# A fused attention and routed feed-forward kernel: expert weights loaded by SyncE and transposed two jobs a step from the start, routing of the first group and scaling of the first tile cut into pieces

## What is computed

```python
q = x + braak_embed[itok][..., None]                 # (32, 256, 256)
attn = softmax(einsum('bsd,btd->bst', q, side))
o = einsum('bst,btd->bsd', attn, side)
t = o * rsqrt(mean(o * o) + EPS) * norm_w            # 8192 tokens
weights = top2_of_8(softmax(t @ gate_w.T))           # renormalised
h1 = t @ w1.T + 2 * lora(t, a1, b1)                  # F = 1024, rank 16, by expert
h3 = t @ w3.T + 2 * lora(t, a3, b3)
act = silu(h1) * h3
out = x + sum_e weights_e * (act @ w2.T + 2 * lora(act, a2, b2))
```

## Time and profile before

| | |
|---|---|
| times of three runs | 1379.82, 1374.30, 1379.27 us, median 1379.27 |
| span of the profiled execution | 1375.7 us |
| PE busy | 1339.7 us (97%) |
| DVE busy | 890.6 us (65%) |
| ACT busy | 545.8 us (40%) |
| POOL busy | 224.0 us (16%) |
| mean granted TensorE clock | 0.993 of full |

### The profile page before, as it was taken

One profiled execution on the slowest core, in us unless ns is written; L12 is line 12 of the kernel. 1 busy time (PEld: TensorE's weight loads), 2 busy tenths in 40 slices (PEclk: granted clock), 3 DMA queues, 4 the chain that ended last, 5 costly groups with the idle time before them and its releaser, 6 DMA issues.

```text
span 1375.7 us, 18571 instructions
## 1 busy us (share of the span) xinstructions
PE 1339.7 (97%) x6660; PEld 1126.7 (82%) x6660; DVE 890.6 (65%) x1552; ACT 545.8 (40%) x1039; POOL 224.0 (16%) x171
## 2 busy tenths in 40 slices
PE   5999999999999999999999999999999999999997
PEld 4999998888788878887888888887888788888885
DVE  2888874665677566756675667656765676565654
ACT  2877773333333333333342334333433333233332
POOL 1334342020202020202020100101111102020200
PEclk8999999999999999999999999999999999999999
DMA  7434461010101101020202010101010101011000
GB/s 235 130 115 138 145 183 49 0 40 32 39 31 33 39 17 52 1 69 0 69 1 69 0 53 16 38 30 38 30 39 30 38 30 39 30 38 32 0 16 16
DMA packets 59278, 68.88 MB, mean 50 GB/s; under 512 B 7003, under 2 KB 46313, under 8 KB 58985
## 3 DMA queue, kind: packets, MB, share of 16 engines
q1 hardware_dynamic: 54088, 63.27, 14.7%
q10 hardware_dynamic: 5152, 5.11, 1.1%
HBM read 51.27 MB, written 17.10 MB: 50 GB/s over the span
## 4 chain that ended last, share of the span: by engine, by line
PE 80%; DVE 9%; issue 6%; ACT 1%; DMA 1%; ACTq 1%; POOL 0%; SPq 0%; POOLq 0%; DVEq 0%
PE bank L1051 25%; PE bank L1053 24%; PE bank L1052 24%; DVE v_full L937 2%; PE bank L1090 2%; DVE act_s L957 2%; PE bank L1129 2%; DVE act_br L953 1%; PE bank L1234 1%; ACTq L562 1%; PE bank L1135 1%; PE bank L1107 1%; DVE act_b L950 1%; DVE br_lo L965 1%; ACT s_hi L668 1%
## 5 line engine op out<-in xcount | busy, mean ns | idle before, releaser
L942 DVE TENSOR_TENSOR act_a<-silu_a,bank 128x512 f32<-128x512 f32 x128 | 87.9, 687 | 181.8 <-PE bank L1053 164.8
L668 ACT ACTIVATE s_hi<-act_s 128x512 fp32r<-128x512 f32 x128 | 80.9, 632 | 257.2 <-DVE act_s L957 256.3
L963 DVE TENSOR_TENSOR s_lo<-act_s,s_hi 128x512 fp32r<-128x512 f32 x128 | 103.7, 810 | 74.4 <-ACT s_hi L668 74.2
L661 ACT ACTIVATE silu_b<-bank 128x512 f32<-128x512 f32 x128 | 76.3, 596 | 185.9 <-PE bank L1053 184.5
L950 DVE TENSOR_TENSOR act_b<-silu_b,bank 128x512 f32<-128x512 f32 x128 | 88.0, 688 | 72.9 <-PE bank L1053 72.0
L515 POOL TENSOR_TENSOR v_lo<-v_full,v_hi 128x512 fp32r<-128x512 f32 x64 | 94.7, 1512 | 130.5 <-ACT v_hi L653 130.5
L657 ACT ACTIVATE silu_a<-bank 128x512 f32<-128x512 f32 x128 | 76.1, 594 | 92.3 <-PE bank L1053 91.1
L957 DVE TENSOR_TENSOR act_s<-act_a,act_br 128x512 f32<-128x512 f32 x128 | 103.2, 807 | 4.4
L504 POOL TENSOR_TENSOR t_lo<-t_scaled,t_hi 128x1024 fp32r<-128x1024 f32 x16 | 38.5, 2406 | 414.4 <-ACT t_hi L649 414.4
L1051 PE MATMUL bank<-t_hi,w1T_hi 128*128 128x512 f32 x256 | 100.6, 393 | 0.8 <-DVE act_b L950 0.8
L1051 PE MATMUL bank<-s_hi,w2T_hi 128*128 128x512 f32 x256 | 100.4, 392 | 0.2 <-DVE br_lo L965 0.2
(11 more groups left out here) (175 smaller groups left out, 3190.5 us busy)
## 6 DMA issues: line engine op xcount, KB each, us to landing
x_in<-in_x SPq DMA_DIRECT2D x32, 256.0 KB, 2.8
kv<-in_fside_BxSxS SPq DMA_DIRECT2D x32, 256.0 KB, 3.1
t_scratch<-oT SPq DMA_DIRECT2D x32, 256.0 KB, 2.1
t_in<-t_scratch SPq DMA_DIRECT2D x16, 512.0 KB
x_out<-in_x SPq DMA_DIRECT2D x16, 512.0 KB, 3.5
out<-x_out SPq DMA_DIRECT2D x32, 256.0 KB, 2.2
rho<-scale_scratch SPq DMA_DIRECT2D x16, 256.0 KB
rstd<-scale_scratch SPq DMA_DIRECT2D x16, 256.0 KB
```

The lines of the kernel that those rows point to most:

```text
L661: nc.scalar.activation(silu_b[:, :], h1_bank[j % 2][:, :], ACT.Silu).then_inc(silu_b_ready, 1)
L668: nc.scalar.activation(s_hi[j % 2][:, :], act_s[j % 2][:, :], ACT.Copy).then_inc(s_hi_ready, 1)
L942: nc.vector.tensor_tensor(act_a[j % 2][:, :], silu_a[j % 2][:, :], h3_bank[j % 2][:, :], ALU.mult).then_inc(act_a_ready, 1)
L963: nc.vector.tensor_tensor(s_lo[j % 2][:, :], act_s[j % 2][:, :], f32(s_hi[j % 2][:, :]), ALU.subtract)
```

## The change

SP issues the weight loads, in between the loads of the first four sequences, in the order in which the jobs use them, each group with its own semaphore. ACT issues only the two small loads for the bias. The twenty jobs stand two a step in steps 0 to 9. HEAD is now steps 0 to 19, the loop 20 to 27. Routing is cut in ten pieces (eight in steps 10 to 17, the weight's in step 19), behind `probT_low`. The row transposes, the copy and **both tile loads** now stand between step 19 and step 20. Tile 0's scaling stands in halves in steps 28 and 29. For sequence 0, kv is transposed ahead of q.

```diff
-            sp.dma_start(itok_in[:, :], itok.partition_broadcast(STAGES)).then_inc(stage_loaded, 16)
-            sp.dma_start(embed_in[:, :], embed).then_inc(stage_loaded, 16)
             load(0, 0, ring_full=False)
...
-            for c in range(1, RING):
-                load(0, c, ring_full=False)
+            load(0, 1, ring_full=False)
+            sp.dma_start(a1_in[:, :], a1.rearrange("e r d -> (e r) d")).then_inc(a13_loaded, 16)
+            sp.dma_start(a3_in[:, :], a3.rearrange("e r d -> (e r) d")).then_inc(a13_loaded, 16)
+            sp.dma_start(w1_in[:, :, :], w1.rearrange("(p j) d -> p j d", j=FC)).then_inc(w1_loaded, 16)
+            load(0, 2, ring_full=False)
+            sp.dma_start(w3_in[:, :, :], w3.rearrange("(p j) d -> p j d", j=FC)).then_inc(w3_loaded, 16)
+            load(0, 3, ring_full=False)
...
             for c in HEAD[1:]:
                 step(0, c)
-            with sp.Fori(0, LOOPS) as g:
-                for c in LOOP:
-                    step(g, c)
...
             sp.wait_ge(wT_ready, JOBS)
             for k in range(2):
-                sp.wait_ge(t_stored[k], 16)
-            load(0, BATCH - 1)
+                sp.wait_ge(t_stored[k], 32)
             store_rows(0)
             load_tile(0, 0, buffers_used=False)
+            load_tile(0, 1, buffers_used=False)
+            with sp.Fori(0, LOOPS) as g:
+                for c in LOOP:
+                    step(g, c)
+            load(0, BATCH - 1)
             store(0, TAIL[0] - 1)
-            load_tile(0, 1, buffers_used=False)
...
             qk_high(0, 0)
-            load_weights()
...
+            def first_transpose_qk():
+                pe.wait_ge(seq_loaded[0], 32)
+                transpose_seq(kv[0], kT_bank)
+                pe.wait_ge(q_ready, 1)
+                transpose_seq(q[0], qT_bank).then_inc(qkT_ready, 1)
...
             def step(g, c, jobs_here=False, peeled=False):
                 row_max(g, c)
-                if jobs_here:
-                    weight_low(c, 0)
-                if peeled:
-                    beside(c)
                 if not isinstance(g, int) or c + 1 < BATCH:
                     qk_low(g, c + 1)
...
                 probT_low(g, c)
-                if jobs_here:
-                    weight_low(c, 3)
+                if jobs_here and c > 0:
+                    weight_low(jobs_of(c)[1])
+                if peeled:
+                    beside(c)
```

More of the change, by code:

```diff
@@ L282, in adaln_moe_ffn @@
                                    dst[1][:, c, j0 * P:(j0 + 4) * P], nw_at(c))]))
-        FIRST_B_JOB = len(jobs)
+        B_JOB = len(jobs)
         for src, dst in ((b1_by_j, b1T), (b3_by_j, b3T)):
@@ L288, in adaln_moe_ffn @@
                                dst[1][:, j0 * P:(j0 + 4) * P], SCALING)]))
+        W2_JOB = len(jobs)
         for j0 in range(0, FC, 2):
@@ L293, in adaln_moe_ffn @@
                            w2T[1][:, j0:j0 + 2].rearrange("p j d -> p (j d)"), 1.0)]))
+        A2_JOB = len(jobs)
         for j0 in range(0, FC, 4):
@@ L297, in adaln_moe_ffn @@
                            a2T[1][:, j0:j0 + 4].rearrange("p j e -> p (j e)"), 1.0)]))
+        B2_JOB = len(jobs)
         jobs.append(([(128 * c, 128, b2_in[:, c].rearrange("p e r -> p (e r)"), P) for c in range(DC)],
@@ L319, in seq @@
             return 4 * g + c
-        T0_STEP = BATCH - 2
-        HEAD, TAIL = range(0, 12), range(28, 32)
-        LOOP = range(12, 16)
+        HEAD, TAIL = range(0, 20), range(28, 32)
+        LOOP = range(20, 24)
+        T0_STEPS = TAIL[0:2]
         LOOPS = (TAIL[0] - LOOP[0]) // 4
@@ L549, in _, with weight_high @@
         def _(act):
[L550 to L566, removed]
+            def weight_high(n):
                 act.wait_ge(wT_ready, n + 1)
@@ L640, in _ @@
                 step(0, c, c in JOB_STEPS)
-                if c == ROUTE_STEP + 2:
+                if c == ROUTE_STEP + 7:
                     exp_gap(0)
-            with act.Fori(0, LOOPS) as g:
-                for c in LOOP:
-                    step(g, c)
             def t_high(g, c):
@@ L720, in _ @@
             copy_rows(0, row_bank, first=True)
+            with act.Fori(0, LOOPS) as g:
+                for c in LOOP:
+                    step(g, c)
             for c in TAIL:
                 step(0, c)
-                if c == T0_STEP:
+                if c == T0_STEPS[-1]:
                     t_high(0, 0)
@@ L839, in route_second, with route_first, newton, rsqrt_seed @@
                 link(r, 15, nc.vector.tensor_tensor(hots[:, 1].rearrange("p e c -> p c e"), g_hot2[:, :, :], g_hot1[:, :, :], ALU.subtract))
-            def route_rstd(r):
+            def route_first(r):
+                route_copy(r)
+                route_hot1(r)
+            def route_second(r):
+                route_rest(r)
+                route_hot2(r)
+                route_hots(r)
+            def newton(r, n):
+                target = scales[:, 1] if n == 2 else g_y[:, :]
+                link(r, 18 + 3 * n, nc.vector.tensor_tensor(g_t[:, :], g_y[:, :], g_y[:, :], ALU.mult))
+                link(r, 19 + 3 * n, nc.vector.scalar_tensor_tensor(g_t[:, :], g_t[:, :], -0.5, g_z[:, :],
+                                                                   ALU.mult, ALU.mult))
+                link(r, 20 + 3 * n, nc.vector.scalar_tensor_tensor(target, g_t[:, :], 1.5, g_y[:, :],
+                                                                   ALU.add, ALU.mult))
+            def rsqrt_seed(r):
                 y_bits, z_bits = g_y[:, :].bitcast(I32), g_z[:, :].bitcast(I32)
@@ L845, in route_rstd @@
                 link(r, 17, nc.vector.tensor_scalar(y_bits, y_bits, -1.0, RSQRT_SEED, ALU.mult, ALU.add))
+            def route_rstd(r):
+                rsqrt_seed(r)
                 for n in range(3):
[L847 to L852, removed]
+                    newton(r, n)
             def route_gap(r):
@@ L869, in scale_t @@
                     dve.wait_ge(t_lo_ready, tile_no(g, c))
[L870 to L874, removed]
             def load_weight(g, c, buffer_used=True):
@@ L1082, in weight_job, with transpose_seq @@
                 last.then_inc(wT_ready, 1)
+            def transpose_seq(src, dst):
+                for dc in range(DC):
+                    for h in range(SC):
+                        last = nc.tensor.transpose(dst[:, dc * S + h * P:dc * S + (h + 1) * P],
+                                                   src[:, h, dc * P:(dc + 1) * P], ident[:, :])
+                return last
             def transpose_qk(g, c):
                 pe.wait_ge(q_ready, seq(g, c) + 1)
[L1087 to L1090, removed]
-                                                       src[:, h, dc * P:(dc + 1) * P], ident[:, :])
-                last.then_inc(qkT_ready, 1)
+                transpose_seq(q[c % 2], qT_bank)
+                transpose_seq(kv[c % RING], kT_bank).then_inc(qkT_ready, 1)
+            def first_transpose_qk():
[3 more added lines that the diff above has]
+                transpose_seq(q[0], qT_bank).then_inc(qkT_ready, 1)
             def scores(g, c):
@@ L1151, in step @@
                 if jobs_here:
-                    weight_job(c, 1)
+                    weight_job(jobs_of(c)[0])
+                if jobs_here and c == 0:
+                    weight_job(jobs_of(c)[1])
                 if c >= 2:
@@ L1171, in _ @@
                 step(0, c, c in JOB_STEPS)
+            pe.wait_ge(w_lo_ready, JOBS)
+            transpose_rows(0, row_bank)
             with pe.Fori(0, LOOPS) as g:
```

151 lines of the change are left out of this document (98 added, 53 removed).

## The result

| | before | after |
|---|---|---|
| median of 13 runs | 1379.82 us | 1386.44 us |
| lowest and highest | 1374.30, 1384.25 | 1385.08, 1392.02 |
| span of the profiled execution | 1375.7 us | 1383.4 us |

The ratio is 1.0056, with a 95% interval of 1.0041 to 1.0072. The kernel is 0.6% slower. The forecast was 1372.2 us and its range ended at 1377.5: the forecast is wrong in sign.

The account below looks back on a forecast made before the run. PE, busy in 97% of the span, was taken as the bound. Gains of 10.9, 2.1 and 5.2 us less 11.1 lost gave 7.1 us less: span 1368.6, median 1372.2 us, range 1364 to 1377.5.

Parts of the forecast that it names:

- four places: PE's idle or low-clock stretches before stage 2: step 0, the clock after it, routing in steps 9 to 11, stage 1's end.
- The start: Steps 0 and 1: ACT freed of weight transfers, jobs filling PE's wait, scores(2) at 22.4; 10.9 us gained.
- rival 2: The start gains little: SP held by its ring, sequence 4 or the weights late; 1377 us, 13 in 100.
- Routing: Steps 9 to 11 before: cut in pieces behind `probT_low`, its delay of 2.3 us mostly goes; 2.1 us gained.
- The stop in the middle: PE waits 8.2 us for sequence 23, queued behind the tile loads, then 2.9 for the low clock; 11.1 us lost.
- Rival 1: Sequence 23 overtakes the tile loads: stop of 3.8 us, gain 11.5, 1367.8 us; 17 in 100.
- rival 3: Slower than before: stop before step 22 over 22 us, broadcast loads at half their rate; 3 in 100.
- R: The start of the row transposes, 186.11 us before, now the end of step 19; sequence 23's landing forecast at R + 20.2.
- The end of stage 1: Tile 0 scaled earlier: the 2.03 us wait and low clock go, low_rank at 207.5 if undisturbed; 5.2 us gained.

Follow-up runs that it names:

- e1: After with 12 more do-nothing instructions (waits already met) at the start of DVE's list; median 1376.31 us, ratio to before 0.9986.
- e2: Before with 84 more instructions on DVE in step 0, its stage 2 loop then placed as in after; median 1390.08 us, ratio to before 1.0080.
- e5: Before with 60 more instructions on DVE in step 0; median 1379.97 us, ratio to before 1.0007.
- e6: Before with 74 more instructions on DVE in step 0; median 1384.68 us, ratio to before 1.0042.
- e3: After with sequence 23 loaded ahead of rows and tile 0, and tile 1's loads moved behind the loop; median 1373.06 us, ratio to before 0.9960.
- e4: After with the edits of e1 and e3 together; median 1362.63 us, ratio to before 0.9886.
- e7: e4 with row transposes, their copy and both tile loads back behind the loop, tile 0 scaled in step 30; median 1366.17 us, ratio to before 0.9900.

## Why the prediction was wrong

**The step that failed** is a term that the sum hasn't got: stage 2 was put at nothing. The prediction counts four places that can give or lose time, "all before stage 2", and the part on the kernel says of stage 2: "The change leaves this stage as it is." No reason is given beyond that. The text of stage 2 is the same, and so is each instruction of it. Its place in DVE's program is not. The forecast counted the instructions that were moved and those queued behind them, and didn't ask where the loop behind them would stand. This cost 10.4 us in after's profile, and e1, e2, e5 and e6 show it to be the place of DVE's loop alone. Without it after would be at 1376.3, inside the range and 4 us above the forecast.

**The start** was right: 9.57, 16.70 and 22.78 where 9.3, 16.8 and 22.4 were forecast. With four jobs done by then the gain is 31.53 + 1.76 - 22.78 = 10.5 (forecast 10.9). Sequence 4's data did come 1 us later than DVE wanted it (landed at 29.2, wanted at 28.3; forecast 25.5 and 27.5): SP was held in issuing by its queue, as ACT had been (two weights' issues took 4.77 and 3.36 us). That is a piece of rival 2, but next to nothing reached PE.

**Routing**: steps of 5.5 us up to 128.76, as forecast.

**The stop in the middle** had the right place, releaser and cause in SP's order; both sizes were low. It was 9.6 us, not 8.2. `t_in` went out 3.2 us behind the row transposes, as forecast, but sequence 23's kv landed 18.3 us behind it, not 17. The clock came back after 7.4 us of work, not 5.8, so it took 3.7 and not 2.9. Together 13.3 us instead of 11.1. Taking it away gives the same: 12.4 us at the mark from after to e3, and 13.9 from e1 (227.53) to e4. Rival 1, by which sequence 23 would overtake the tiles (a stop of 3.8 us), did not come true. But the sentence under it, "A transfer waits for what was issued on its queue ahead of it", doesn't hold as it stands. Sequence 24's `x_in`, issued at 144.38, landed 5.96 us later at 150.34, and sequence 23's kv, issued ahead of it at 143.09, 7.64 us later at 150.73. So what the Trainium skill says (DMA: Bandwidth & Descriptors, "Queues, rings and completion order"), that a later transfer may complete before an earlier one of its issuer, is seen in this trace; it didn't help sequence 23. When the tiles' own loads landed, the trace doesn't record. In rival 3, the landings for a stop of 15.3 and of 22 us are R + 27.3 and R + 34, with the 0.7 us of DVE that the forecast's own stop has; the chance doesn't hang on it.

**The end of stage 1**: no stop, and full clock, as forecast. Low_rank began 212.70 - 208.53 = 4.2 us earlier, where the sum has 7.1. The missing 2.9 us are 2.2 of the stop, 0.4 of the start, and 0.3 that is spread over the rest. One sign of it: from the probabilities of step 29 to those of step 30 it is 6.12 us (197.36 to 203.48), where a plain step takes 5.52.

**The end of the kernel**: 1.6 us, since PE's clock was low in four of the last six matmuls and in the last transposes. e1 has this too (1.94 us); before, e2, e3, e4, e5 and e6 have not. It doesn't go with the stop in the middle: e7 has no such stop, and its last six matmuls ran at the low clock as well (0.63 us each behind the first). Why the clock falls there in some executions isn't settled; no run tests it.

**The range and the chances.** Slower had 3 in 100, all for a stop of 22 us. An unnamed effect on the stage whose text is untouched had none. The change moved 84 instructions ahead of a loop, and so a share for "something else is shifted" was due.

## What to carry to other kernels

When a change writes out more steps ahead of a hot loop, count the instructions ahead of it, in the built program (here DVE's; no other engine's list was tested), and see whether the body still lies in as few fetch blocks as before. The sign in the profile is idle time marked "issue" at the first instruction of each turn but the first, with more packets on the engine's instruction queue; the remedy cost twelve instructions that do nothing. And before a block of broadcast loads goes into a queue, look for the next plain load that has a due time. Here that load ahead of the block, with half of the block moved to a later place, was worth 13.4 us; the two weren't tried apart. Together with the twelve instructions it makes a kernel 1.1% faster than before.

## What the runs showed of the hardware

- In turns whose jump back went with more packets on the instruction queue, DVE stood 2.4 us behind the jump, and 1.7 us more at a border three or four instructions behind its target (after). With the border ten instructions further on, only the first showed (e6). DVE stands 1.4 us there in any case, so on PE's path this was 2.1 us and 1.0 us a turn.
- The same 276 instructions brought 3 to 6 packets on the instruction queue in 890 us with two blocks (before, e5, e1), and 29 to 31 with three (e2, e6, after).
- PE's clock rose after 7.4 us of work at 1.2 GHz behind a stop of 9.6 us in after, and after 4.9 us behind one of 9.06 us in before.
- Of two loads on SP's queue in after, the one issued 1.3 us later landed 0.4 us earlier (150.34 and 150.73).
